# Graph attention and routed feed-forward: attention weights leave PSUM once as fp32, values are summed in column bands, and the lists of the node loop hold offsets

## What is computed

```python
q = (layernorm(x) @ Wq.T + bq).reshape(512, 8, 16)
k = (msg @ Wk.T + bk); v = (msg @ Wv.T + bv)      # msg = h_neigh + E[edge_types]
scores = einsum('bhd,bnhd->bhn', q, k) / 4
scores = where(adj == 0, -1e9, scores)
attn = softmax(scores); attn = where(adj == 0, 0, attn)
x = x + einsum('bhn,bnhd->bhd', attn, v) @ Wo.T + bo
# feed-forward on layernorm(x): at each of 8 levels
score = einsum('td,td->t', h, w1s[current]) + b1s[current]
out += (einsum('td,tdo->to', h, w2s[current]) + b2s[current]) * gelu(abs(score))
current = current * 2 + (score > 0) + 1
```

## Time and profile before

| what | us |
|---|---|
| median of three runs (150.55 to 155.39) | 151.63 |
| the profiled execution: its time / its span | 151.52 / 149.7 |
| TensorE busy in the span | 119.4 |
| VectorE busy | 110.2 |
| ScalarE busy | 77.7 |

### The profile page before, as it was taken

One profiled execution on the slowest core, in us unless ns is written; L12 is line 12 of the kernel. 1 busy time (PEld: TensorE's weight loads), 2 busy tenths in 40 slices (PEclk: granted clock), 3 DMA queues, 4 the chain that ended last, 5 costly groups with the idle time before them and its releaser, 6 DMA issues.

```text
span 149.7 us, 3466 instructions
## 1 busy us (share of the span) xinstructions
PE 119.4 (80%) x952; PEld 82.6 (55%) x953; DVE 110.2 (74%) x305; ACT 77.7 (52%) x179; POOL 42.2 (28%) x84
## 2 busy tenths in 40 slices
PE   6975499499989889865999749978979789889930
PEld 2351354456556556553755417356868577777820
DVE  1779868995999999987488899436645697676660
ACT  3076679756899899895216001543434433344520
POOL 2401504910000000000030003704544525686562
PEclk9998557965999999999599985799999999999996
DMA  4969999999999400000020000200000000010001
GB/s 123 309 226 419 420 420 420 431 416 429 437 468 427 198 4 0 0 4 0 2 70 4 0 0 0 53 18 7 0 2 2 0 0 0 0 35 0 0 0 35
DMA packets 3420, 20.14 MB, mean 134 GB/s; under 512 B 465, under 2 KB 2000, under 8 KB 2896
## 3 DMA queue, kind: packets, MB, share of 16 engines
q1 hardware_dynamic: 2048, 18.42, 29.9%
q10 hardware_dynamic: 1104, 1.05, 2.3%
q0 software_dynamic: 256, 0.52, 1.2%
HBM read 19.47 MB, written 0.52 MB: 133 GB/s over the span
## 4 chain that ended last, share of the span: by engine, by line
PE 49%; DVE 21%; issue 13%; ACT 10%; DVEq 3%; POOL 1%; ACTq 0%; POOLq 0%
PE s_ps L765 9%; PE turn_ps L620 5%; PE turn_ps L765 5%; DVE prob L917 5%; ACT prob L454 5%; PE s_ps L589 4%; PE s_ps L533 4%; ACT prob_t L450 4%; PE s_ps L548 4%; DVE early L823 3%; PE s_ps L688 2%; PE misc_ps L543 2%; DVE w L823 2%; PE aux_ps L765 2%; DVEq L80 2%
## 5 line engine op out<-in xcount | busy, mean ns | idle before, releaser
L620 PE MATMUL turn_ps<-ident,prob 128*128 128x128 f32 x128 | 23.4, 311 | 9.0 <-ACT prob L454 7.4
L382 POOL TENSOR_TENSOR early<-early,scaled_sb 128x128 f32<-128x128 f32 x48 | 21.3, 456 | 23.4 <-ACT scaled_sb L516 23.0
L454 ACT ACTIVATE prob<-prob,negmax 128x512 f32<-128x512 f32 x32 | 23.1, 721 | 6.6 <-DVE negmax L917 6.1
L924 DVE TENSOR_TENSOR prob_t<-turn_ps,prob_t 128x512 f16<-128x512 f32 x32 | 22.1, 690 | 5.9 <-ACT prob_t L450 5.6
L620 PEld LDWEIGHTS turn_ps<-ident,prob 128*128 128x128 f32 x128 | 15.3, 155 | 19.6 <-ACT prob L454 17.3
L917 DVE CUSTOM_DVE_ANT_0 prob<-s_ps,mask 128x512 f32<-128x512 f32 x32 | 21.8, 682 | 1.2 <-PE s_ps L589 0.7
L450 ACT ACTIVATE prob_t<-turn_ps 128x512 f16<-128x512 f32 x32 | 18.6, 581 | 2.2 <-PE aux_ps L603 1.5
L1056 DVE SCALAR_TENSOR_TENSOR early<-s_ps,coef,early 128x128 f32<-128x128 f32 x48 | 14.1, 346 | 7.3 <-PE s_ps L765 4.6
L765 PE MATMUL s_ps<-w,msg 128*128 x128 | 18.4, 286 | 0.9 <-DVE early L1056 0.5
L589 PE MATMUL s_ps<-early 32*128 32x512 bf16 x96 | 15.3, 430 | 2.5 <-DVE early L823 2.4
L765 PEld LDWEIGHTS s_ps<-w,msg 128*128 128x128 f32 x128 | 15.6, 191 | 2.6 <-issue 2.3
(11 more groups left out here) (173 smaller groups left out, 196.2 us busy)
## 6 DMA issues: line engine op xcount, KB each, us to landing
w<-in_w_t SPq DMA_DIRECT2D x3, 4096.0 KB, 22.7
w<-in_w_t SPq DMA_DIRECT2D x1, 4032.0 KB, 22.4
w<-in_adj SPq DMA_DIRECT2D x1, 1024.0 KB, 8.6
w_sb<-in_w_t ACTq DMA_DIRECT2D x1, 384.0 KB, 4.3
x_sb<-in_x SPq DMA_DIRECT2D x1, 256.0 KB, 3.2
msg<-in_neigh_t SPq DMA_DIRECT2D x1, 256.0 KB, 4.0
x_rows<-x ACTq DMA_DIRECT2D x1, 256.0 KB, 2.3
row_sb<-in_rows ACTq DMA_DIRECT2D x1, 255.5 KB, 7.1
```

What stands on the lines that cost most here:

```text
L382: nc.gpsimd.tensor_tensor(mine, mine, scaled_sb[:, i, :], ALU.add).then_inc(pooled[i], STEP)
L454: nc.scalar.activation(prob[:, u % RING, :], prob[:, u % RING, :], ACT.Exp, bias=negmax[:, t, h:h + 1], scale=-1.0, accum_out=psums[:, t, ...
L620: last = nc.tensor.transpose(turn_ps[u % 2][:, m * P:(m + 1) * P], prob[:, u % RING, m * P:(m + 1) * P], ident[:])
L924: nc.vector.tensor_tensor(prob_t[:, v % 2, 1, :], turn_ps[v % 2][:], prob_t[:, v % 2, 0, :], ALU.subtract).then_inc(lo_moved, 1)
```

## The change

The attention weights are copied once from `turn_ps` as fp32, for even units by ScalarE and for odd ones by VectorE, to one of eight `slots` (six of them in `spare`, two in `prob_t`). The values are no longer split: `v_st` holds 32 fp32 columns for a head, 16 of values, one of ones, 15 of zeros; GpSimd fills the constant part at the start. The product is turned round: the values are the weights (128 x 32) and the fp32 attention block is the moving data (128 x 128). Four heads, a `quad`, write four bands of 32 partitions of one bank, and one quarter of the sum over the neighbours is made for each of them in a step (`weighted_values(quad, m)`), three to five units behind. The row sum of the exponentials comes out as the 17th column, and the exponential's accumulated output is gone. Once a tile, ScalarE copies the 128 x 256 result (`values_out`), TensorE turns it back by two transposes (`values_back`), and VectorE divides by the sums (`normalise_values`).

The first group of two tiles is turned for Wo before the last tile is finished. The load of the Gelu table stands later on ScalarE. The last quarter of `w2` waits for the end of the attention, since `slots` occupy its place.

In the node loop the lists hold 128 times the node number. TensorE loads the eight entries of a turn at its head (`list_entries`) and uses them as they are; VectorE and ScalarE keep their registers and loads, and divide by 128.

```diff
 def node_at(engine, entry, j):
-    return engine.snap(entry[(j + HALF) % STEP], min_val=0, max_val=NODES)
+    return engine.snap(entry[(j + HALF) % STEP], min_val=0, max_val=NODES * D) // D
+
+def list_entries(nc, engine, nodes, at):
+    at = nc.s_assert_within(at, 0, TILES * NODES_PAD - STEP,
+                            skip_runtime_bounds_check_because="at is a multiple of STEP inside the lists")
+    _, found = nc.values_load_multi_w_load_instructions(
+        nodes[0:1, bass.ds(at, STEP)], engines=(engine,), min_val=0, max_val=NODES * D,
+        skip_runtime_bounds_check_because="entries are D times node numbers, D times NODES past the list's end")
+    return found
...
-        v_st = sb("v_st", [P, NT, HEADS, PARTS, DH], BF16)
+        v_st = sb("v_st", [P, NT, HEADS, V_COLS])
-        prob_t = sb("prob_t", [P, 2, 2, N_NEIGH], F16)
+        prob_t = sb("prob_t", [P, 2, N_NEIGH])
...
                 if n0 == SPLIT_AT:
-                    sp.wait_ge(mask_ready, 2)
...
+                    sp.wait_ge(summed, UNITS // QUAD)
...
+            nc.gpsimd.memset(v_st[:], 0.0).then_inc(v_room, 1)
+            pool.wait_ge(v_room, 1)
+            nc.gpsimd.memset(v_st[:, :, :, DH:DH + 1], 1.0).then_inc(v_room, 1)
...
+            def values_out(t):
+                act.wait_ge(summed, 2 * (t + 1))
+                nc.scalar.activation(o_t[:, (t % 2) * 2 * P:(t % 2 + 1) * 2 * P], o_ps[t % 2], ACT.Copy
+                                     ).then_inc(o_out, 1)
             for u in range(UNITS + LAG):
-                if u >= LAG:
-                    v = u - LAG
+                v = u - LAG
+                if v >= 0 and v % 2 == 0:
                     act.wait_ge(turned, v + 1)
-                    if v >= 2:
-                        act.wait_ge(summed, v - 1)
-                    nc.scalar.activation(prob_t[:, v % 2, 0, :], turn_ps[v % 2][:], ACT.Copy).then_inc(hi_moved, 1)
+                    if v >= SLOTS:
+                        act.wait_ge(summed, (v - SLOTS) // QUAD + 1)
+                    nc.scalar.activation(slots[v % SLOTS], turn_ps[0][:], ACT.Copy).then_inc(moved[0], 1)
...
-                                         bias=negmax[:, t, h:h + 1], scale=-1.0,
-                                         accum_out=psums[:, t, h:h + 1]).then_inc(exped, 1)
-                if u == 0:
-                    value_part(1)
+                                         bias=negmax[:, t, h:h + 1], scale=-1.0).then_inc(exped, 1)
...
+                if u >= 13 and (u - 13) % HEADS == 0:
+                    values_out((u - 13) // HEADS)
+            values_out(TILES - 1)
...
                 nc.scalar.activation(nodes[:, 0:TILES * NODES_PAD], s_ps[0:1, 0:2, :].rearrange("p a n -> p (a n)"), ACT.Copy,
-                                 bias=float(NODES)).then_inc(lists_ready, 1)
+                                 bias=float(NODES * D), scale=float(D)).then_inc(lists_ready, 1)
...
+            def weighted_values(quad, m):
+                t, g = divmod(quad, 2)
+                if m == 0:
+                    for i in range(2):
+                        pe.wait_ge(moved[i], 2 * (quad + 1))
...
+                for j in range(QUAD):
+                    h = g * QUAD + j
+                    last = nc.tensor.matmul(o_ps[t % 2][j * V_COLS:(j + 1) * V_COLS, g * P:(g + 1) * P],
+                                            v_st[:, m, h, :], slots[(quad * QUAD + j) % SLOTS][:, m * P:(m + 1) * P],
+                                            start=(m == 0), stop=(m == NT - 1))
+                if m == NT - 1:
+                    last.then_inc(summed, 1)
+
+            def values_back(t):
+                pe.wait_ge(o_out, t + 1)
+                for g in range(2):
+                    lo = ((t % 2) * 2 + g) * P
+                    last = nc.tensor.transpose((aux_ps, misc_ps)[t % 2][:, (2 + g) * P:(3 + g) * P],
+                                               o_t[:, lo:lo + P], ident[:])
+                last.then_inc(o_back, 1)
...
+                if u >= QUAD + 1:
+                    weighted_values(*divmod(u - QUAD - 1, NT))
+                if u >= 14 and (u - 14) % HEADS == 0:
+                    values_back((u - 14) // HEADS)
                 pe.wait_ge(exped, u + 1)
                 if u >= 2:
-                    pe.wait_ge(lo_moved, u - 1)
+                    pe.wait_ge(moved[u % 2], moved_before(u)[u % 2])
...
-                if u >= LAG:
-                    weighted_values(u - LAG)
                 if u in LATE:
                     scores(u // 2 + 1)
-            for u in range(UNITS - LAG, UNITS):
-                weighted_values(u)
+            for step in range(UNITS - QUAD - 1, UNITS):
+                weighted_values(*divmod(step, NT))
+            pe.wait_ge(o_moved, GROUPS[0][1])
+            transposes(turn_ps[0], o_sb, o_turned, *GROUPS[0])
+            values_back(TILES - 1)
             pe.wait_ge(consts2, 10)
+            keep_busy(2)
             pe.wait_ge(o_moved, TILES)
-            keep_busy(4)
-            for i, (t0, t1) in enumerate(GROUPS):
-                pe.wait_ge(o_ready, i + 1)
-                transposes(turn_ps[i], o_sb, o_turned, t0, t1)
+            transposes(turn_ps[1], o_sb, o_turned, *GROUPS[1])
...
             def products(s, e, at):
+                found = list_entries(nc, pe.engine, nodes, at)
                 for j in range(STEP):
-                    if j == HALF:
-                        entries_ahead(nc, nc.tensor, entry, nodes, at)
...
                     nc.tensor.matmul(product_ps[j], hs_t[:, s * P:(s + 1) * P],
-                                     w2[:, bass.ds(node_at(nc.tensor, entry, j), 1), :
-                                        ].rearrange("p n o -> p (n o)"), start=True, stop=True
+                                     w2_flat[:, bass.ds(found[j], D)], start=True, stop=True
                                      ).then_inc(multiplied[j], STEP)
...
+            def normalise_values(t):
+                dve.wait_ge(o_back, t + 1)
+                nc.vector.tensor_scalar(psums[:, t, :], back_ps[t % 2][:, :, DH], TINY, None, ALU.max
...
+                nc.vector.reciprocal(psums[:, t, :], psums[:, t, :]).then_inc(o_scaled, 1)
...
+                                        psums[:, t, :].unsqueeze(2).to_broadcast([P, HEADS, DH]), ALU.mult
+                                        ).then_inc(o_moved, 1)
...
-                if u >= LAG:
-                    v = u - LAG
-                    dve.wait_ge(hi_moved, v + 1)
-                    nc.vector.tensor_tensor(prob_t[:, v % 2, 1, :], turn_ps[v % 2][:], prob_t[:, v % 2, 0, :],
-                                            ALU.subtract).then_inc(lo_moved, 1)
...
+                v = u - LAG
+                if v >= 0 and v % 2 == 1:
+                    dve.wait_ge(turned, v + 1)
+                    if v >= SLOTS:
+                        dve.wait_ge(summed, (v - SLOTS) // QUAD + 1)
+                    nc.vector.tensor_copy(slots[v % SLOTS], turn_ps[1][:]).then_inc(moved[1], 1)
+                if u >= 15 and (u - 15) % HEADS == 0:
+                    normalise_values((u - 15) // HEADS)
+            normalise_values(TILES - 1)
```

More of the change, by code:

```diff
@@ L46 @@
 LAG = 2
+QUAD = 4
+SLOTS = 2 * QUAD
+V_COLS = 32
+TINY = 1e-30
 LATE = (2, 6)
@@ L201, in gnn_ffn_kernel @@
         idle = early[:, 0, :].bitcast(BF16)[:, 0:N_NEIGH]
-        v_f = o_sb[:].rearrange("p t d -> p (t d)")
+        slots = [spare[:, lo // D:(lo + N_NEIGH) // D, :].rearrange("p a n -> p (a n)") for lo in (0, 7168)
+                 ] + [prob_t[:, i, :] for i in range(2)
+                      ] + [spare[:, lo // D:(lo + N_NEIGH) // D, :].rearrange("p a n -> p (a n)")
+                           for lo in (512, 1024, 1536, 2048)]
         perm = view(prob[:], 0, TILES * N_TOK, F16, "p (t s) -> p t s", s=N_TOK)
@@ L296, in _ @@
                 if n0 == SPLIT_AT:
-                    sp.wait_ge(mask_ready, 2)
-                    for g in range(SIDE):
-                        sp.wait_ge(k_first[g], 2)
-                        sp.wait_ge(k_third[g], 1)
-                    for part in range(len(Q_SLICES)):
-                        sp.wait_ge(q_second[part], 1)
-                        sp.wait_ge(q_mixed[part], 1)
-                        sp.wait_ge(q_third[part], 1)
+                    sp.wait_ge(summed, UNITS // QUAD)
                 sp.dma_start(w2[:, n0:n1, :], w2_t[:, n0 * D:n1 * D].rearrange("p (n o) -> p n o", o=D)
@@ L592, in scores @@
                             ins.then_inc(scored, 1)
[L594 to L607 removed]
+            def weighted_values(quad, m):
[3 more added lines that the diff above has]
+                        pe.wait_ge(moved[i], 2 * (quad + 1))
+                    if quad == 0:
+                        pe.wait_ge(v_ready, 1)
+                    if quad == 2:
+                        pe.wait_ge(q_moved[1], SIDE)
+                    if g == 0 and t >= 2:
+                        pe.wait_ge(o_moved, t - 1)
+                for j in range(QUAD):
```

(8 more changed lines are left out.)

92 lines of the change are left out of this document (28 added, 64 removed).

## The result

| | before | after |
|---|---|---|
| median of four runs | 153.15 | 144.83 (144.63 to 153.54) |
| ratio to before | | 0.958, 95% interval [0.950, 0.967] |
| profiled execution: time / span | 151.52 / 149.7 | 144.79 / 142.9 |

A forecast was written before the change was run, and what follows sets the result against it. VectorE was taken to set the pace before, TensorE after. 151.52 - 1.3 (start) + 4.3 (steady part) + 0.9 (clock) + 0.3 (end) + 0 (node loop) = 155.7 us, 155.5 for the median; range 145 to 161.

The forecast's parts named there:

- The step that failed: Attention loop: a step of V, four fp32 products of two records each, takes 5 x 0.112 = 0.56 us on TensorE.
- The rival of side by side: Attention loop: all four column bands run at once, V 0.25 us, a pair 2.47, total 146.6 us; chance 0.27.
- the rival without overlap: Attention loop: column bands run one after another, V 0.90 us, a pair 3.77, total 165 us; chance 0.17.
- The steady part: T of unit 8 to T of unit 31: 11.5 pairs at 3.1 us plus 0.9 for `values_back`, +4.3 us.
- the 0.9 for the clock: Attention loop: an allowance of 0.9 us out of 3.2 lost if a slow-clock stretch of 6.8 us comes again.
- The changes of form: TensorE in the attention loop: five switches between full, row-band and column-band products a pair, 0.09 us each, two before.
- VectorE and ScalarE: Attention loop: VectorE falls to 2.01 us a pair and ScalarE to 1.8 to 2.0, both from 2.6 to 2.8.
- The start: Up to the mask of unit 8: VectorE drops the remainders, -1.3 us, bounds 0 and -2.1.
- The clock: Granted TensorE clock in the attention loop: a coin toss; a slow stretch makes a TensorE-bound pair 5.8 us instead of 3.1.
- The end: T of unit 31 to the first product with Wo: 5.78 us instead of 5.48, +0.3, with four steps of V at 1.90.
- The node loop: Sixteen turns: TensorE's saved loads against VectorE's division, -0.20 to +0.20 us a turn, -3 to +3 in all, taken as 0.
- Hidden, as forecast: Last quarter of `w2`, Gelu table load and GpSimd's memset: each stands beside other work and costs nothing.

The follow-up runs named there:

- The three orders: The kernel after (144.83 us median), and it with a step of V in one column band (165.53 us) or in two bands (151.30 us).
- The two steps in one go: The kernel after with both steps of V of a pair made together on even units: 146.1 us median (144.79 to 147.27).
- the run with two bands: The kernel after with a step of V making two quarters for two heads, instead of one quarter for four: 151.30 us (one run).
- all three edits: The kernel after with two steps of V together on even units, a second list for TensorE, and the query's second part made by VectorE: 141.06 us median.
- filling the hole: The kernel after with eight idle fp32 products on TensorE between T of unit 4 and the first step of V: 144.67 us median (144.51 to 145.01).
- the old loop: The kernel after with the node loop of before: 149.68 us median; with the eight idle products as well, 143.31 to 147.13 us.
- the last version: The kernel after with all three edits and GpSimd's add held back until the query's third part: 140.06 us median; with five idle products too, 140.33.
- the profile with two lists: The kernel after with VectorE and ScalarE reading node numbers and only TensorE offsets, from a second list: 149.7 us median (143.15 to 153.61).

## Why the prediction was wrong

**The step that failed** is "The second record of a band has to wait for the first, since it uses the same columns, while the first record of the next band can go with it if products start in order: 5 x 0.112 = 0.56. I take this." The order was wrong. All four first records go together, then all four second ones: 0.13 + 0.11 = 0.24 us a step, not 0.56. The three orders show it: 8, 4 and 2 rounds at 0.11. The first half of the sentence was right (four products on the same columns took eight rounds) and even accounts for the two rounds. What failed is that the next band was thought to stand behind the second record of the one ahead. The rows of S, which spoke for side by side, were the better witness. It was worth 23 x 0.32 = 7.4 us, most of the 10.9 between forecast and result. The rival of side by side, 146.6 us, was right in its mechanism and within 2 us, but partly by luck: the changes of form were dearer than it had them, and the next paragraph's miscount made up for half of that. Its end is also summed wrongly: eight rounds in place of 17 are 9 x 0.112 less and not 12, so -0.7 for -1.2; measured is -0.6. (The end of the rival without overlap leaves out its own 0.3.)

**The steady part** was forecast at 32.2 + 4.3 + 0.9 = 37.4 us and took 29.85. Besides the 7.4 of V and the 0.9 for the clock, which was not lost, a second mistake is in it: it counts 11.5 pairs with S, but between T of unit 8 and T of unit 31 only ten S stand, as the last units have none ahead of them. A pair without S is 0.75 shorter, which makes 1.1. Against these three the dearer changes of form took back 11.5 x 0.17 = 2.0.

**The changes of form** exist, as forecast, but are dearer: the pair has 2.64 - 0.66 - 0.88 - 0.48 = 0.62 for five, not 0.45. By starts, S to V leaves 0.09, V to T 0.12 and T to V or S 0.15; the last two are longer than the 0.09 of the earlier trace rows. The two steps in one go collected 0.11 each on the average.

**VectorE and ScalarE** went to slack as forecast. Their terms were off without effect: the exponential without accumulated output takes 711 ns (721 before), at the dear end of the 0.60 to 0.72 forecast, and the copy of VectorE 688, not 650.

**The start.** Forecast -1.3, measured -2.5. One omission is shown: "the value parts were beside this path". In the trace of before an operation of the keys took 1.70 us while GpSimd's part of the value split ran from 14.23 for 1.16; after, the same operation takes 0.74:

```profile
14.23 1.70 DVE L823 SCALAR_TENSOR_TENSOR early<-w,from_odd 128x512 bf16<-128x512 bf16 x1
...
14.23 1.16 POOL L327 TENSOR_TENSOR row_room<-row_room,v_st 128x512 f32<-128x512 f32 x1 [7.27 <-ACT v_st L432]
```

That gives 0.96. Against it the mixed product of the query rose from 1.27 to 2.41, since it now starts together with GpSimd's subtraction. Mask 0 came 0.36 earlier, but it lies between 13.25 and 13.83 in runs whose start is the same. The start's half clock lasted 6.8 us, to 21.8, instead of 10.2, to 24.0. That counts: in the run with two bands it lasted 10.2 (12.4 to 22.6), as before, and there the mask of unit 8 came at 30.59, 1.5 earlier than before, although its steps of V are longer. So 1.5 of the 2.5 or somewhat more are the change's, near the 1.3 forecast, and the rest most likely goes with the clock. It is not taken apart further. The 0.8 from mask 8 to T of unit 8 goes with the clock: that stretch was at 0.50 before, from 30.8 on the earlier trace rows, and at 1.00 after. So, most likely, does the 1.1 between Wo and the node loop, where the mean granted clock (last but two of the columns) was 0.83 before and 0.94 after (and in the profile of all three edits, with 0.88, this stretch took 28.1):

```profile
72.50:99.90 27.40, 23.45 (x156) 13.49 (x156) 20.83 (x79) 6.27 (x13) 5.47 (x6) 0.83 0.07 20
```

```profile
66.20:92.50 26.30, 21.25 (x156) 12.27 (x154) 20.74 (x79) 7.75 (x14) 5.46 (x6) 0.94 0.41 158
```

**The clock** was rightly called a coin toss, and rightly dearer for a kernel bound by TensorE: half clock from 28 us costs 5.8 us up to T of unit 31 (one execution), and the eleven runs of the kernel after reach 9% above the lowest, while all 44 of before lie within 4% (149.66 to 155.39). The profiled execution didn't meet it, so the 0.9 wasn't lost. The forecast treated the toss as given.

Does filling the hole help? Of the runs of the unfilled versions (the kernel after and six edits of it) 14 of 43 lie over 2% above the lowest of their own kernel, of the filled ones 1 of 19. Kernel for kernel it is 4 of 11 against 0 of 6 (the kernel after), 3 of 4 against 1 of 7 (the old loop) and 1 of 6 against 0 of 6 (the last version). The count is rough: the version with two steps in one go counts with 0 of 4, though its profile had half clock for 13.7 us. And the series differ: beside the 3 of 4 the kernel before had four of seven over 2%, beside the 0 of 6 one of ten. In the profiles, of nine unfilled ones with the hole at full clock four fell to half behind it and five did not; of three filled ones none fell. The profile with two lists lost its clock in another way: it was at half from 12.8 on, long before the hole. So filling may well help, but it is not shown, and what tips an execution stays open.

**The end.** Forecast +0.3, measured -0.6: four steps of V in one go take 1.08 us by their merged line, not 1.90. It is the same error once more.

**The node loop.** Forecast 0, measured +0.6. The two sides were named, TensorE's saving and VectorE's division, and bounded at 0.05 a value each; measured are 16 ns saved (53 to 37) and 46 lost (67 to 113). The small sum hides two larger parts: TensorE's offsets alone bring the loop from 49.6 to 50.0 down to 47.7 to 48.8, and the division takes it to 50.2 to 50.4.

**Hidden, as forecast:** the last quarter of `w2` (it starts at 63.96 us and lands in 14.1), the load of the Gelu table, GpSimd's memset of `v_st`.

## What to carry to other kernels

Count TensorE's time for fp32 products in column bands in rounds, as here: the largest number of records in any band, at 0.11 us for a record of 128 columns, plus a gap of 0.09 to 0.15 us at each change of form; the usual pair took 2.64, 3.05 and 3.91 us with four bands, two and one. So spread neighbouring products over all bands and keep steps of one form together. Where an engine is to gain from a new format of shared data, ask what every other reader pays for it: a second copy of the list (loop 47.7 us) was cheaper than one division on a queue that sets the pace (50.4). When VectorE's work reads two tensors in SBUF, look at what GpSimd runs beside it (here 2.41 us instead of 1.01, ending 0.82 behind GpSimd's), and when a wait on GpSimd's queue is taken away, at everything that was queued behind it.

## What the runs showed of the hardware

- The two records of an fp32 product didn't block other column bands: first records of four bands started within 0.02 us, second ones 0.13 later.
- Four fp32 products in four column bands took two rounds, 0.13 + 0.11 = 0.24 us; all in one band they took eight of 0.11. Within a round the third record started 0.01 to 0.02 us behind the first.
- VectorE operations with two inputs in SBUF took 0.74 (128 x 512) and 1.01 us (128 x 768) alone, 1.70 to 1.76 and 2.41 when they started with a GpSimd operation of 1.16 to 1.65 us that reads SBUF. They ended 0.55 and 0.82 us behind it, whether they started with it or 1.2 us into it. One that had started 0.27 us ahead (15.86, before) kept its 0.74, and GpSimd's took 1.48 instead of 1.16.
- A register division took 46 ns more on VectorE's queue (67 to 113) and 37 on ScalarE's (53 to 90).
- At the same hole of 2 us, TensorE's granted clock stayed at 1.00 in one execution of the kernel after and fell to 0.50 for 13.6 us in another. With the hole filled six runs lay within 0.5 us; that the filling did it is not shown.
